# Row maxima per half of the queries: a hybrid layer's attention on one Trainium2 core

## The chip, the cores and the metric

The kernel runs on one core of one Trainium2 chip (trn2). The metric is the time of one execution on the device in microseconds. Engine names are those of the profile: PE multiplies matrices, DVE is the vector engine, ACT the scalar engine, POOL GpSimd, SP the engine that issues nearly all DMAs.

## What is computed

A residual stack over x of shape (2, 1024, 128): a gated linear recurrence with an MLP, a mixture of experts, an attention with a relative bias, and the same mixture again. Each takes the layer-normed x and is added to it. The change touches the attention, which has 16 heads of 8 channels (D = 128, scale 128 ** -0.5):

```python
q, k, v = (x @ W.T, split into 16 heads of 8, for Wq, Wk, Wv)
attn = softmax(q k^T * scale, axis=-1)
attn = attn + rel_bias_table[i - j + seq_len - 1]   # clipped to the table
out = attn @ v
out = (out - mean(out)) * rsqrt(var(out) + eps) * ln_gamma + ln_beta
```

## The kernel before, in words

Every engine has an instruction list of its own, written out by hand; semaphores order them. The first 200 us are dense layers. Then the attention runs in GROUPS = 8 groups of GH = 4 heads (four for each of the NB = 2 rows of the batch). Within a group the S = 1024 queries and keys are NT = 8 tiles of 128, and TH = 4 tiles make a half of 512.

Queries and keys are split into three bf16 parts each (L992 to L1005 on DVE, L637 on ACT, L528 on POOL), stored to `qk_scratch` (`store_parts`, L414) and loaded again, stacked to 72 rows (`load_products`, L423, 24 DMAs for a group: a query load L429 and a key load L430 for each of four heads and three parts), into one of BUFS = 3 buffers.

**Maxima.** For each head and query tile PE multiplies 128 queries by all 1024 keys into two PSUM banks (`max_item`, L1331, two matmuls of 512 columns, L1339), and DVE reduces them to minus the maximum (L1028). A group has MAXES = 32 of these. One transpose turns the 128 x 32 of them (`turn_maxes`, L1343), DVE splits them into three bf16 parts (`split_negmax`, L1030), and SP loads these as rows 72 to 74 under the queries (`load_negmax`, L432, three DMAs, L436), so that the scores come out with the maximum taken off.

**Scores.** A group has STEPS = 16 steps: two halves q of the queries, eight key tiles t in each. A step (`step`, L1420) is four score matmuls, one for each head (`scores`, L1393, L1402), with the exponentials on ACT (L731), and the weighing of the step before (`weigh`, L1405, L1416), which adds up in one bank. After eight steps ACT takes that bank (`take_pv`, L718, L721). The first score of a group waits for `negmax_loaded`.

**The ring.** Maxima, turns, the bias products (`bias_part`, L1347, L1353), their turn (`turn_bias`, L1357) and the output's turn (`turn_out`, L1362, eight transposes) share two PSUM slots of two banks each, in the order of the list RING (L190, 36 items); PE fills, DVE empties in the same order (`empty`, L1046). An item waits until the item two before it is emptied, a turn also until the last of its maxima is (`ring_needs`, L209). An item is (kind, d, k): it belongs to the group d after the one whose scores run. Share j of RING, `j * 36 // 16` to `(j + 1) * 36 // 16`, goes into step FIRST + j, FIRST = 2, so shares 14 and 15 lie in steps 0 and 1 of the next group. RING starts with maximum 10 of the next group; its turn is item 25, followed by maxima of the group after next (d = 2) up to EARLY = 10, and the output's turn is last. Ahead of the first score there are RING_AHEAD's 43 items (32 maxima of group 0, a turn, 10 maxima of group 1), between which the attention's projections of row 1 are placed (L1460 to L1477 on PE, L1076 to L1099 on DVE). Groups 6 and 7 run over shortened lists, since no further group follows: group 7 has no maxima beside it.

**SP's queue** (`round_`, L444) is, for each group G: wait until step 1 is scored, load the products of G + 2; wait for the bias table to be free, load that of G + 2; wait for the split maxima of G + 1, load them. SP works strictly in this order, as every engine does.

**Row 0's norm** after the attention (`attended_out`, `attended`, L1106 to L1125) runs on DVE at the end of group 6's list, and the mixture of row 0 begins beside group 7 (TURN_STEP, LOGITS_STEP, X_STEP, L206).

Of the kernel before, what the change touches and what calls it, by code (L numbers as in the profile page):

```python
# [28 lines left out]
BF16 = mybir.dt.bfloat16  # L29
ALU = mybir.AluOpType  # L30
# [76 lines left out]
def values(b):  # L107
    return [(f"V.{b}.{h}", "dve") for h in range(2)] + [(f"CS.{b}", "dve")]
# [73 lines left out]
MAXES = GH * NT  # L182
# [15 lines left out]
BIAS_AT = RING.index(("bias", 0, 0))  # L198

RING_BEFORE_LAST = [item for item in RING if item[1] < 2]  # L200
RING_LAST = [item for item in RING if item[1] < 1]

TURN_STEP, LOGITS_STEP, X_STEP = 4, 5, 10  # L206


def ring_needs(items, k):  # L209

    kind, d, _ = items[k]
    made_from = {"turn": ("max", d, MAXES - 1), "bias_turn": ("bias", d, 0)}.get(kind)
    return max(k - 1, items.index(made_from) + 1) if made_from in items else k - 1


def build(nc, x_in, out, w, tab):
    ctx = ExitStack()
    with ctx:
# [99 lines left out]
        qs = q_words.bitcast(BF16).rearrange("p (n h t) -> p n h t", n=BUFS, h=GH)  # L318
# [10 lines left out]
        nm_rest = sb("nm_rest", [GH * NT, P])  # L329
        nm_part = sb("nm_part", [GH * NT, NPART, P], BF16)  # L330
        rl = sb("rl", [P, NT, GH])
# [10 lines left out]
        def score_bank(g, n):  # L342
# [26 lines left out]
        PER_GROUP = {ring_filled: len(RING), ring_emptied: len(RING), negmax_split: 1, scores_filled: STEPS * GH,  # L369
                     exp_done: STEPS * GH, pv_done: STEPS, pv_out: 2, varying_ready: 1, v_ready: 1, negmax_loaded: 16 * NPART,  # L370
# [3 lines left out]
        RING_SHORT = len(RING) - len(RING_BEFORE_LAST)  # L374

        def at(G, s, k):

            short = RING_SHORT if s in (ring_filled, ring_emptied) and isinstance(G, int) and G == GROUPS - 1 else 0
            return G * PER_GROUP[s] + k + AHEAD.get(s, 0) - short
# [1170 lines left out]
```

## Time and profile before

| | |
|---|---|
| median of 3 runs | 740.3 us (738.14 to 742.24) |
| profiled execution, span | 738.4 us |
| PE busy | 666.5 us (90%) |
| DVE busy | 533.7 us (72%) |
| ACT busy | 381.2 us (52%) |
| POOL busy | 104.9 us (14%) |
| first score of the attention | 256.2 us from the span's start |
| last take of weighed values (L721) | 664.0 us |

The span is from the first to the last instruction of one execution that the hardware profiler recorded; its time as a run is not given apart from that; the lowest of the timed runs is 738.14 us. Busy time is the union of an engine's instructions. Matmuls are pipelined and their ends are modelled, so a busy PE is not PE at its peak. In a view of groups the idle time before a group's instructions stands last, with what ended most of it. In a timeline, a row merges instructions that follow each other on one engine; DMA-issuing instructions on SP's queue are shown as SPq. PEclk is the granted share of PE's 2.4 GHz.

### The profile page before, as it was taken

How to read it: one execution, taken by the hardware profiler on the slowest of the kernel's cores; microseconds unless marked ns; L12 is line 12 of the kernel's file. 1: busy time of each engine (PE TensorE's matmuls, PEld its weight loads, DVE VectorE, ACT ScalarE, POOL GpSimd, SP SyncE). 2: the span in 40 equal slices, each digit the busy share in tenths (PEclk: the TensorE clock that was granted, in tenths of full speed). 3: DMA queues.
4: the chain of work that ended last, by engine and by line, in shares of the span. 5: the costliest groups of instructions: out<-in, count | busy, mean ns of one | idle time of the engine just before them, and what ended most of it. 6: DMA issues, size and time to landing. Idle time of an engine off the chain costs nothing.

```text
span 738.4 us, 10515 instructions
## 1 busy us (share of the span) xinstructions
PE 666.5 (90%) x3192; PEld 254.5 (34%) x3192; DVE 533.7 (72%) x956; ACT 381.2 (52%) x687; POOL 104.9 (14%) x100
## 2 busy tenths in 40 slices
PE   3988898999777699999999899999999998988997
PEld 1434344444343222332322232332322322324443
DVE  5379788746699868868878768868788688308744
ACT  2745133333203057767767657766667677882231
POOL 5910110001044411020020020020100202002000
PEclk9998899999969789999999999999999999999999
DMA  8000000000313102012012020030120000000000
GB/s 253 5 1 0 1 0 1 1 0 0 112 67 122 58 28 95 2 41 83 4 56 66 17 83 28 18 99 9 32 91 3 2 0 2 2 1 0 1 28 28
DMA packets 21413, 26.59 MB, mean 36 GB/s; under 512 B 3312, under 2 KB 12016, under 8 KB 21360
## 3 DMA queue, kind: packets, MB, share of 16 engines
q1 hardware_dynamic: 20496, 25.39, 10.8%
q8 instruction: 29, 0.48, 0.3%
q0 software_dynamic: 144, 0.52, 0.2%
q14 instruction: 24, 0.20, 0.1%
q10 hardware_dynamic: 720, 0.00, 0.1%
HBM read 21.52 MB, written 4.19 MB: 35 GB/s over the span
## 4 chain that ended last, share of the span: by engine, by line
PE 69%; DVE 19%; ACT 4%; issue 2%; DMA 2%; DVEq 1%; POOL 1%; SPq 1%; POOLq 0%; ACTq 0%
PE banks L1416 17%; PE banks L1339 15%; PE banks L1402 14%; PE banks L1154 6%; DVE negmax L1028 6%; PE banks L1224 4%; PE banks L1265 3%; PE banks L1353 2%; PE banks L1215 2%; PE banks L1161 2%; DVE arena L886 1%; ACT arena L731 1%; DVE arena L936 1%; DVE stats L783 1%; PE banks L1366 1%
## 5 line engine op out<-in xcount | busy, mean ns | idle before, releaser
L1028 DVE TENSOR_REDUCE negmax<-banks 128x1 f32<-128x1024 f32 x256 | 300.8, 1217 | 68.6 <-PE banks L1339 67.4
L731 ACT ACTIVATE arena<-banks 128x512 f32<-128x512 f32 x512 | 271.7, 601 | 144.1 <-PE banks L1402 140.6
L1339 PE MATMUL banks<-arena 72*128 72x512 bf16 x512 | 161.3, 400 | 23.6 <-DVE negmax L1028 19.7
L1402 PE MATMUL banks<-arena 75*128 75x512 bf16 x512 | 160.2, 384 | 6.7 <-ACT arena L731 3.1
L1416 PE MATMUL banks<-arena 128*32 128x512 f32 x1024 | 138.1, 612 | 0.7 <-ACT arena L731 0.7
L1339 PEld LDWEIGHTS banks<-arena 72*128 72x128 bf16 x512 | 37.8, 100 | 163.0 <-DVE negmax L1028 77.0
L1402 PEld LDWEIGHTS banks<-arena 75*128 75x128 bf16 x512 | 48.6, 98 | 95.7 <-ACT arena L731 48.0
L495 POOL TENSOR_TENSOR rstd<-veps,neghalf 128x4 f32<-128x4 f32 (+1 forms) x24 | 27.1, 1129 | 247.3 <-DVE veps L802 192.1
L1224 PE MATMUL banks<-arena,bT 128*128 128x512 f32 x128 | 60.1, 593 | 1.6 <-ACT arena L585 1.6
L585 ACT ACTIVATE arena<-banks 128x512 f32<-128x512 f32 (+1 forms) x56 | 32.2, 595 | 53.1 <-PE banks L1154 22.7
L886 DVE TENSOR_SCALAR arena<-banks,bi 128x512 f32<-128x512 f32 x32 | 23.8, 745 | 34.7 <-PE banks L1224 34.7
L562 POOL TENSOR_TENSOR pause<-neghalf 128x8 f32<-128x8 f32 x7 | 1.4, 199 | 309.9 <-PE banks L1353 309.9
L1224 PEld LDWEIGHTS banks<-arena,bT 128*128 128x128 f32 x128 | 24.2, 190 | 32.2 <-issue 29.9
L1416 PEld LDWEIGHTS banks<-arena 128*32 128x32 f32 x1024 | 20.3, 108 | 39.3 <-issue 33.2
L1215 PE MATMUL banks<-hT,wiT 128*128 128x512 f32 x64 | 32.9, 615 | 0.0
L1161 PE MATMUL banks<-ident,nt 128*128 128x128 f32 x80 | 13.7, 313 | 20.4 <-DVE nt L812 11.9
L546 POOL TENSOR_TENSOR arena<-arena,t_last 128x2048 f32<-128x2048 f32 x8 | 28.8, 3599 | 0.0
L585 ACT ACTIVATE hT<-banks 128x512 f32<-128x512 f32 x12 | 6.8, 596 | 31.8 <-PE banks L1161 31.8
L1265 PE MATMUL banks<-arena,woT 128*128 128x512 f32 x48 | 22.1, 597 | 0.3
L585 ACT ACTIVATE x<-banks,bi 128x512 f32<-128x512 f32 x16 | 11.0, 687 | 20.3 <-PE banks L1224 20.3
L783 DVE BATCH_NORM_STATS2 stats<-x 128x6 f32<-128x128 f32 x80 | 17.4, 280 | 5.4 <-DMA x<-in_x 4.5
L585 ACT ACTIVATE oT<-banks,bo 128x512 f32<-128x512 f32 x8 | 5.5, 687 | 30.4 <-PE banks L1265 30.4
(128 smaller groups left out, 614.1 us busy)
## 6 DMA issues: line engine op xcount, KB each, us to landing
arena<-qk_scratch SPq DMA_DIRECT2D x192, 48.0 KB
arena<-in_tab SPq DMA_DIRECT2D x8, 1024.0 KB, 6.8
qk_scratch<-arena SPq DMA_DIRECT2D x8, 384.0 KB, 2.8
out<-x SPq DMA_DIRECT2D x4, 256.0 KB, 2.3
x<-in_x SPq DMA_DIRECT2D x1, 512.0 KB, 4.5
x<-in_x POOLq DMA_DIRECT2D x1, 512.0 KB, 7.7
arena<-nm_part SPq DMA_DIRECT2D x24, 8.0 KB, 1.9
w_aT<-in_w_aT SPq DMA_DIRECT2D x1, 256.0 KB, 6.5
```

Source lines behind the costliest of these rows:

```text
L546: pool.tensor_tensor(varying, bias_raw[:, :, ::-1], t_last[:, bass.ds(G * GH, GH)].unsqueeze(2).broadcast_to([P, GH, BIASW]), ALU.subtract ...
L585: act.activation(dst, banks[:, BANK[name], :], func, **kw).then_inc(signal or act_emptied, 1)
L731: act.activation(probs[s % 2][:, h, :], score_bank(g, n), ACT.Exp, scale=SCALE).then_inc(exp_done, 1)
L886: dve.tensor_scalar(h1[:, c % 2, :], bank(name), bi[:, c:c + 1], 0.0, ALU.add, ALU.max).then_inc(dve_emptied, 1)
L1028: return dve.tensor_reduce(negmax[:, buf, k:k + 1], slot.rearrange("p a b -> p (a b)"), axis=AXX, op=ALU.max, negate=True)
L1154: last = pe.matmul(banks[:, BANK[name], :], lhsT, rhs, start=i == 0, stop=i == len(terms) - 1)
L1215: pe.matmul(banks[:, BANK[name], :], chunk(wiT, c), half(hT[:, b], h), start=True, stop=False, skip_group_check=True)
L1224: pe.matmul(banks[:, BANK[name], :], chunk(bT, c), half(moe[b][4][:, k, :], h), start=False, stop=k == 1, skip_group_check=True).then_inc( ...
L1265: last = pe.matmul(banks[:, BANK[name], :], woT[:, c, :], moe[b][2][h][:, c, :], start=c == 0, stop=c == FC - 1)
L1339: last = pe.matmul(slot[:, half_, :], qs[0:STACK, buf, h, t * P:(t + 1) * P], ks[0:STACK, buf, h, half_ * HALF:(half_ + 1) * HALF], start= ...
L1402: pe.matmul(score_bank(g, n), ks[0:DEPTH, g % BUFS, h, t * P:(t + 1) * P], qs[0:DEPTH, g % BUFS, h, q * HALF:(q + 1) * HALF], start=True, ...
L1416: last = pe.matmul(pv_bank[32 * h:32 * h + VW, :], vpg[:, g % BUFS, t, h, :], probs[s % 2][:, h, :], start=t == 0, stop=t == NT - 1)
```

## The change

The maxima of a group are taken, turned, split and loaded for each half of the queries: MAXES is 16, and item k of 32 is maximum `k % 16` of half `k // 16`. Each group has two turns of 128 x 16, two splits and two times three loads. The first score of each half waits for its own loads. The queries lie as (half, head, 512) in their buffer, and the query loads write two pieces of 1 KB a row instead of one of 2 KB. The second half's maxima of a group from EARLY = 8 on, and its turn, are now beside that group's own scores (d = 0); no item has d = 2. RING has 38 items, RING_AHEAD 25. The output is turned in two halves (items 33 and 37). In SP's order the second half's loads stand behind the product loads. Groups 6 and 7: group 6 has the whole list, group 7 has eight maxima, a turn, the bias and the outputs, three items a step; row 0's norm is done tile by tile between their items. The value copies of the projections go from DVE to ACT, and POOL clears `vpg` and copies the first values ahead of its low parts.

```diff
-MAXES = GH * NT
+MAXES = GH * TH
-EARLY = 10
+EARLY = 8
-NEXT_MAXES = [("max", 1, k) for k in range(EARLY, MAXES)]
-AFTER_NEXT = [("max", 2, 0), ("turn", 1, 0)] + [("max", 2, k) for k in range(1, EARLY)]
-RING = NEXT_MAXES[:4] + [("bias", 0, 0), NEXT_MAXES[4], ("bias_turn", 0, 0)] + NEXT_MAXES[5:] + AFTER_NEXT + [("out", 0, 0)]
-RING_AHEAD = [("max", 1, k) for k in range(MAXES)] + AFTER_NEXT
-BESIDE_FIRST = EARLY - 4
-R_BEFORE, V0_BEFORE, CS0_BEFORE = 2, (4, 5), 7
-TURN_BEFORE, QK_BEFORE, V_BEFORE, CS_BEFORE = 12, (14, 16, 18, 20), (22, 24), 27
+def maxes(d, q, start, stop):
+    return [("max", d, q * MAXES + k) for k in range(start, stop)]
+TURN_0 = maxes(1, 0, 0, 1) + [("turn", 0, 1)] + maxes(1, 0, 1, 3) + BIAS + maxes(1, 0, 3, 4) + BIAS_TURN + maxes(1, 0, 4, MAXES)
+AFTER_TURN = maxes(1, 1, 0, 1) + [("turn", 1, 0)] + maxes(1, 1, 1, EARLY)
+RING = maxes(0, 1, EARLY, MAXES) + TURN_0 + AFTER_TURN[:6] + [("out", 0, 0)] + AFTER_TURN[6:] + [("out", 0, 1)]
+RING_AHEAD = maxes(1, 0, 0, MAXES) + AFTER_TURN
+BESIDE_FIRST = 4
+R_BEFORE, V0_BEFORE, CS0_BEFORE = 2, (3, 4), 5
+TURN_BEFORE, QK_BEFORE, V_BEFORE, CS_BEFORE = 8, (10, 11, 12, 13), (14, 15), 17
+RING_LAST = maxes(0, 1, EARLY, MAXES - 1) + BIAS + maxes(0, 1, MAXES - 1, MAXES) + BIAS_TURN + [("turn", 0, 1), ("out", 0, 0), ("out", 0, 1)]
+LAST_BESIDE = 3
-TURN_STEP, LOGITS_STEP, X_STEP = 4, 5, 10
+TURN_STEP, LOGITS_STEP, X_STEP = 8, 9, 14
...
-            def load_negmax(G, buf):
-                sp.wait_ge(negmax_split, at(G, negmax_split, 1))
+            def load_negmax(G, buf, q):
+                sp.wait_ge(negmax_split, at(G, negmax_split, q + 1))
                 for i in range(NPART):
...
                     sp.wait_ge(scores_filled, at(G, scores_filled, FIRST * GH))
                     load_products(G + 2, (n + 2) % BUFS)
+                load_negmax(G, n % BUFS, 1)
+                if left >= 2:
                     sp.wait_ge(varying_ready, at(G, varying_ready, 2))
                     load_bias(G + 2)
                 if left >= 1:
-                    load_negmax(G + 1, (n + 1) % BUFS)
+                    load_negmax(G + 1, (n + 1) % BUFS, 0)
...
             store_parts(1)
+            load_negmax(0, 0, 0)
+            sp.wait_ge(qk_stored[1], 64)
             sp.wait_ge(varying_ready, 1)
             load_bias(1)
-            load_negmax(0, 0)
...
-                if n == 0:
-                    pe.wait_ge(negmax_loaded, at(G, negmax_loaded, 16 * NPART))
+                if s % NT == 0 and h == 0:
+                    pe.wait_ge(negmax_loaded, at(G, negmax_loaded, (s // NT + 1) * 16 * NPART))
...
+            def round_before_last():
+                G = GROUPS - 2
+                for k, item in enumerate(RING):
+                    dve.wait_ge(ring_filled, at(G, ring_filled, k + 1))
+                    empty(G, G, item, ring_slot(k))
+                    if k in (TH, 2 * TH):
+                        stats_half(N_OUT, 0, o_tok, k // TH - 1)
+                    if NT < k <= 2 * NT:
+                        if k == NT + 1:
+                            dve.drain()
+                        centred(0, k - NT - 1)
...
+                act.activation(v_all[:, b * NG:(b + 1) * NG, h * TH:(h + 1) * TH, :],
+                               banks[:, BANK[name], :].rearrange("p (t g c) -> p g t c", g=NG, c=GW), ACT.Copy).then_inc(act_emptied, 1)
```

## Rows read from the trace of the kernel before

**Rows 1.** The page: span, and busy time, share and instructions of two engines.

```profile
span 738.4 us, 10515 instructions
...
PE 666.5 (90%) x3192; PEld 254.5 (34%) x3192; DVE 533.7 (72%) x956; ACT 381.2 (52%) x687; POOL 104.9 (14%) x100
```

**Rows 2.** The reductions' group: count, busy, mean ns, idle before, releaser.

```profile
L1028 DVE TENSOR_REDUCE negmax<-banks 128x1 f32<-128x1024 f32 x256 | 300.8, 1217 | 68.6 <-PE banks L1339 67.4
```

**Rows 3.** Timeline, PE, steady stretch: start, length, line, op.

```profile
350.79 1.06 PE L1416 MATMUL banks<-arena 128*32 128x512 f32 x8
...
353.63 1.06 PE L1416 MATMUL banks<-arena 128*32 128x512 f32 x8
...
356.61 1.07 PE L1416 MATMUL banks<-arena 128*32 128x512 f32 x8
```

**Rows 4.** Timelines: first score of step 8 (group 2); seven takes.

```profile
387.73 0.60 PE L1402 MATMUL banks<-arena 75*128 75x512 bf16 x2
...
363.50 0.60 ACT L721 ACTIVATE arena<-banks 128x512 f32<-128x512 f32 x1
...
390.25 0.60 ACT L721 ACTIVATE arena<-banks 128x512 f32<-128x512 f32 x1
...
414.22 0.60 ACT L721 ACTIVATE arena<-banks 128x512 f32<-128x512 f32 x1
...
444.85 0.60 ACT L721 ACTIVATE arena<-banks 128x512 f32<-128x512 f32 x1
...
570.25 0.60 ACT L721 ACTIVATE arena<-banks 128x512 f32<-128x512 f32 x1
...
620.23 0.60 ACT L721 ACTIVATE arena<-banks 128x512 f32<-128x512 f32 x1
...
664.03 0.60 ACT L721 ACTIVATE arena<-banks 128x512 f32<-128x512 f32 x1 [1.19 <-PE banks L1416]
```

**Rows 5.** Timeline of SP's queue, groups 1 and 2.

```profile
356.27 1.86 SPq L436 DMA_DIRECT2D arena<-nm_part  x3
...
367.23 0.82 SPq L429 DMA_DIRECT2D arena<-qk_scratch  x1
...
388.53 0.39 SPq L441 DMA_DIRECT2D arena<-in_tab  x1
```

**Rows 6.** The turn in group 1; time to landing of nm_part loads.

```profile
354.62 0.28 PE L1345 MATMUL banks<-ident,negmax 128*32 128x128 f32 x1
...
DMA to landing us min/median/max: 1.8/1.9/3.2
```

**Rows 7.** Windows, last columns PEclk, DMA share, GB/s: product loads; three nm_part loads.

```profile
373.00:387.00 14.00, 13.55 (x98) 4.40 (x98) 8.88 (x10) 8.22 (x17) 4.09 (x3) 1.00 0.18 58
...
357.00:359.00 2.00, 2.00 (x14) 0.52 (x7) 2.00 (x3) 1.12 (x4) 0.00 (x0) 1.00 0.06 12
```

**Rows 8.** PE after a gap of 2.29 us; PEclk in two windows.

```profile
420.91 0.39 PE L1402 MATMUL banks<-arena 75*128 75x512 bf16 x1 [2.29 <-issue]
...
422.00:424.00 2.00, 2.00 (x10) 0.25 (x10) 0.99 (x1) 1.07 (x2) 0.00 (x0) 0.51 0.19 54
...
260.00:262.00 2.00, 2.00 (x6) 0.68 (x5) 1.89 (x3) 0.97 (x2) 0.00 (x0) 0.50 0.00 0
```

**Rows 9.** Timelines of the stage ahead of the scores, 210 to 256 us.

```profile
210.05 6.22 POOL L524 TENSOR_SCALAR nt<-x,mv,rstd 128x128 f32<-128x128 f32 x8
...
229.49 7.70 SPq L419 DMA_DIRECT2D qk_scratch<-arena  x4
...
237.08 0.68 DVE L1009 COPY x<-banks 128x512 f32<-128x512 f32 x1
...
256.17 0.59 PE L1402 MATMUL banks<-arena 75*128 75x512 bf16 x1 [1.09 <-DMA arena<-nm_part]
```

**Rows 10.** Timeline of DVE in the last group: norm work of row 0.

```profile
612.97 0.87 DVE L783 BATCH_NORM_STATS2 stats<-z 128x6 f32<-128x128 f32 x4
...
615.92 2.18 DVE L1112 SCALAR_TENSOR_TENSOR nt<-z,mv,gamma 128x128 f32<-128x128 f32 x8
```

More of the change, by code:

```diff
@@ L1092, in _ @@
                 rest(1, k)
-            for h in range(2):
-                empty_ahead(done, V_BEFORE[h])
-                done = V_BEFORE[h]
-                take_values(1, h)
-            empty_ahead(done, CS_BEFORE)
+            empty_ahead(done, CS_EMPTY)
             take_sum(1)
-            empty_ahead(CS_BEFORE, len(RING_AHEAD))
-            def round_items(G, g, items, first=0):
-                for k, item in enumerate(items, first):
+            empty_ahead(CS_EMPTY, len(RING_AHEAD))
@@ L1103, in round_items @@
+            def round_items(G, g, items):
+                for k, item in enumerate(items):
                     dve.wait_ge(ring_filled, at(G, ring_filled, k + 1))
                     empty(G, g, item, ring_slot(k))
-            def attended_out(b):
-                dve.drain()
-                for h in range(2):
-                    stats_half(N_OUT, b, o_tok, h)
-                for t in range(NT):
-                    dve.scalar_tensor_tensor(out=nt[:, b, t, :].rearrange("p (g c) -> p g c", g=NG), in0=tile_of(o_tok, b, t),
-                                             scalar=mv[:, b, t, 0:1], in1=gamma[:].rearrange("p (g c) -> p g c", g=NG),
-                                             op0=ALU.subtract, op1=ALU.mult)
@@ new lines, in last_round @@
+            def last_round():
+                G = GROUPS - 1
+                dve.wait_ge(x_beta, 1)
+                for k, item in enumerate(RING_LAST[:LAST_OUT]):
+                    dve.wait_ge(ring_filled, at(G, ring_filled, k + 1))
+                    empty(G, G, item, ring_slot(k))
+                    if k < NT:
+                        attended_tile(0, k)
+                norm(N_FFN1, 0, x)
+                route(1, 0)
+                for k in range(LAST_OUT, len(RING_LAST)):
+                    dve.wait_ge(ring_filled, at(G, ring_filled, k + 1))
+                    empty(G, G, RING_LAST[k], last_slot(k))
@@ L1360, in turn_bias, with turn_out @@
                 return last
-            def turn_out(G, slot):
-                pe.wait_ge(pv_out, at(G, pv_out, 2))
-                for t in range(NT):
-                    last = pe.transpose(slot[:, t // TH, (t % TH) * P:(t % TH + 1) * P], chunk(pvT, t), ident[:])
+            def turn_out(G, slot, q):
+                pe.wait_ge(pv_out, at(G, pv_out, q + 1))
+                for t in range(TH):
+                    last = pe.transpose(slot[:, 0, t * P:(t + 1) * P], chunk(pvT, q * TH + t), ident[:])
                 return last
@@ L1435, in step, with beside @@
                     fill_item(k)
-            def beside(items, j):
-                share = RING[j * len(RING) // STEPS:(j + 1) * len(RING) // STEPS]
-                return [items.index(x) for x in share if x in items]
+            def beside(j):
+                return list(range(j * len(RING) // STEPS, (j + 1) * len(RING) // STEPS))
             def round_(G, g, items):
@@ L1447, in round_ @@
                     s = FIRST + j
-                    step(G + s // STEPS, g + s // STEPS, s % STEPS, fill_item, beside(items, j))
+                    step(G + s // STEPS, g + s // STEPS, s % STEPS, fill_item, beside(j))
             for name in LAST_IN_RING:
@@ L1486, in _ @@
                     round_(i * BUFS + n, n, RING)
-            round_(GROUPS - 2, GROUPS - 2, RING_BEFORE_LAST)
+            round_(GROUPS - 2, GROUPS - 2, RING)
             G = GROUPS - 1
             def fill_last(k):
-                fill_round(G, G, RING_LAST, k)
+                pe.wait_ge(ring_emptied, at(G, ring_emptied, ring_needs(RING_LAST, k)))
+                fill(G, G, RING_LAST[k], last_slot(k))
             for j in range(STEPS - FIRST):
                 s = FIRST + j
-                step(G, G, s, fill_last, [j] if j < 2 else [])
+                step(G, G, s, fill_last, list(range(j * LAST_BESIDE, min((j + 1) * LAST_BESIDE, LAST_OUT))))
                 if s == TURN_STEP:
-                    pe.wait_ge(ring_emptied, at(G, ring_emptied, 2))
+                    pe.wait_ge(ring_emptied, at(G, ring_emptied, LAST_OUT))
                     flip_norm(N_FFN1, 0, "T1")
```

145 lines of the change are left out of this document (75 added, 70 removed).

## The prediction

> **What bounds the kernel now.** I read the page first: in the profiled execution of 738.4 us PE is busy 90% and DVE 72% [rows 1]. Those are averages over stages with different limits, so I then went through timelines. The group of the reductions shows what DVE does with its share: 256 maxima of 1.22 us each, 300.8 us [rows 2]. In the middle of a group of heads the bursts of weighing (L1416) stand 2.84 us apart, and 2.98 us where the turn lies between them [rows 3]. A step there holds four scores and two items of maxima, eight matmuls of 512 columns, 1.7 us at 2.4 GHz, and the burst, close to 1 us: PE is full. ACT needs 4 x 0.6 us for it and DVE two maxima; neither is the bound. A group takes 50.7 us: 26.8 us from the take of step 0 to that of step 8 (the bias products lie in this half), 24.0 us for the other half; group 3 is 3.9 us longer in its first half, 30.6 us [rows 4]. Ahead of the first score DVE reduces 42 maxima without a pause, and PE waits on it: that stage is DVE's.
>
> **SP's queue** is what the change leans on. It issues the 24 loads of products for group 2's successor but one from 367.23 to 388.53, 21.3 us, 0.89 us each, and is then free for the next thing [rows 5]. The three loads of split maxima come 1.65 us after the turn on PE; issuing them takes 1.9 us, a load lands 1.9 us after its issue, so the last one is there about 3.15 us after the first issue [rows 5, 6]. Before the change they start at 356.27, eleven microseconds ahead of the products, and nobody waits for them.
>
> **The change, part by part.**
>
> *Shorter stage ahead of the scores.* The list falls from 43 items to 25, 18 reductions less. DVE also loses four value copies of 0.68 us [rows 9] to ACT, which idles there; behind them on ACT stand the turns of row 1, not ready before POOL has finished its norm at 216.3 [rows 9], and for row 1 nothing but the first exponentials. The limit by DVE alone is 18 x 1.22 + 2.7 = 24.7 us. But the chain of row 1 remains. Its turn stands at item 8 instead of 12 and so starts about 4 us earlier; between its four products stands one maximum instead of two, 3 x 1.2 = 3.6 us less. SP's last store of parts, finished at 237.2 [rows 9], moves to about 229.5. The value sum, two maxima, the turn and the split follow, 3 us, then 3.15 us of loads, and about 1 us for the stores still in flight (the slowest landing of such a load is 3.2 us against 1.9 [rows 6]): the first score comes at 236.5 instead of 256.2, 19.7 us earlier. POOL's clearing and its first two value copies move ahead of its low parts, into time in which it waited for these. On SP the first loads of maxima move ahead of the wait for the stores and of the table load, which takes that wait off the path. The first two steps carry four items instead of six at the low clock: 2 x 2 x 512 columns at 1.2 GHz are 1.7 us, of which I take 1.3. Sum -21, bounds -25 and -13 (the chain of row 1 not shortened at all).
>
> *The second half's loads behind the products.* In SP's order the loads of the second half's maxima stand behind the 24 product loads of the group after next. These start, now as before, when step 1 has been scored. Step 8 needs the maxima. In group 2 step 8's first score came at 387.95 (the second matmul of the row at 387.73 [rows 4]), 20.7 us after the first product load; the new order has one item more before it but only half of an output turn, the same within 0.3 us. The maxima are there after 21.3 + 3.15 = 24.5 us. PE, whose queue is in order, stands for about 4.0 us at that score, with every item, weighing and exponential behind it. Groups 0, 1, 2, 4 and 5 pay this; group 3 has 3.9 us more in the loop's turn-round, so 0.3 us; groups 6 and 7 load no products. Behind the loads of maxima SP has the table load, which POOL needs only a group later, so nobody waits for that. 5 x 4.0 + 0.3 = +20.3. Bounds per group: 3.2 (a queue 0.8 us faster) and 5.3 (the landing of 3.2 us).
>
> *The clock.* After a gap of 2.29 us on PE the granted clock of 422 to 424 us is 0.51, that is 1.2 GHz, with the engine full [rows 8]. That half group lost 3.9 us: the gap and some 1.5 us for the clock. A gap of 4 us should do no less: 5 x 1.5 = +7.5. Bounds 0 and 3.4 each: at the start the clock stays at 0.50 although PE is full [rows 8], and 1.2 steps of 2.84 us run at half the clock take 3.4 us more.
>
> *Work moved to the last two groups.* The 18 maxima come back in groups 6 and 7 (50.0 and 43.8 us now [rows 4]). PE is the bound there or nearly so, an item is two times 512 columns at 2.4 GHz, 0.43 us: 7.7 us. In group 7 three maxima share a step, with a tile of the norm behind each (2.18 us for eight [rows 10]): DVE needs 4.2 us for such a step, about 1 us more than PE, twice. The norm of row 0, until now 10 us of DVE between the groups' items, is strewn over groups 6 and 7 (four statistics are 0.87 us, eight tiles 2.18 us [rows 10]) and takes the slack that DVE has there; its turn and logits stand four steps later, still ahead of the end of group 7. Sum +9.5, bounds 7.7 and 14.
>
> *In each of seven groups* there is one turn more and the output turn is in two: 0.15 us for a turn [rows 3], the same for the split of the output. The turn of the first half now stands two steps ahead of its use instead of three: 5.7 us against 1.65 + 3.15 and a reduction in front, so no slack; 0.2 us. 7 x 0.5 = +3.5, bounds 0 and 10. *The last output* in two halves puts 0.6 us on the tail (-0.3 to 1).
>
> Sum: -21 + 20.3 + 7.5 + 9.5 + 3.5 + 0.6 = +20.4 on the execution of 738.4 us. The runs' median, 740.3, stands 1.9 us above it, so 760.7, rounded to 761.
>
> **A rule that bears on it.** The product loads hold the DMA share at 0.18 for 14 us on end, with nothing else moving [rows 7]; 3 of 16 engines are 0.19. They seem to use three engines only, and to fill them. The Trainium skill says that an outermost dimension of size c below 16, such as a leading broadcast, confines a DMA to at most c engines (DMA: Bandwidth & Descriptors, Rules for kernel authors); by that rule, the trace agrees. That gives a rival. A packet of 2 KB costs 0.18 x 14 x 16 / (15.8 loads x 24) = 0.106 us of one engine; the 96 small packets of the three loads of maxima 0.06 x 2 x 16 / 96 = 0.02 us each [rows 7]. The query loads now have 48 pieces of 1 KB instead of 24 of 2 KB. On the line between both rows 1 KB costs 0.057 us, and a pair of loads 1.76 us on three engines against 1.78 us of issue: just hidden, which I take. At 0.106 us for 1 KB too it is 2.54 us a pair, and after 12 pairs 9 us of backlog lie in front of the maxima.
>
> **The rivals.** *Three engines back up* (chance 0.12): for it, they are full today; against it, small packets are cheap in the rows. Half of the 9 us in five groups and a little in group 3: 761 + 24 = 785, up to 810.
>
> *The maxima arrive in time* (0.13), and the kernel gets faster. The place is SP's queue in groups 0 to 5; it decides at 17.5 us for the 24 product loads, 0.73 us each. Then +20.3 and +7.5 drop out: 761 - 27.8 = 733. For it speaks only that the issue itself is shown as 0.82 us at most and that the rest of the 0.89 us may be address arithmetic; against it, this pitch holds in every group seen.
>
> *The stage ahead does not get shorter as counted* (0.08): row 1's chain through POOL, ACT, DVE and SP bounds it from the start; the first score comes at 245, and the time is 769. *The stall is there but cheap* (0.05): no clock loss and the full 25 us at the start, 744 and less.
>
> **How the numbers follow.** The forecast gets 0.62: its stall is a matter of order in one queue, and its own range is 748 to 774. From 743 to 785 the range takes in the third rival and half of the backed-up engines; left out are the arrival in time (0.13) and the rest of the backlog (0.06). A measurement of this kernel can tell some 0.5% from no change, 3.7 us. Faster 0.13, the arrival in time; same 0.05, the cheap stall; slower 0.82.
>
> **What would show it.** First score near 236. In the waits, PE's scores released by the loads of nm_part, 4 us in five groups and nearly nothing in the fourth. In SP's queue, the three loads of maxima directly behind the 24 of products, once a group, and three more later. PEclk at 0.5 for some us after each gap. First halves of 32 us instead of 26.8. If first halves stay at 27, my step on SP's queue is wrong, and the kernel is faster.

## The result, and the profile after

The kernel got slower: 786.8 us median of 4 runs (784.08 to 794.84) against 739.56 us for the kernel before in the same runs (738.14 to 742.24), a ratio of 1.064, 95% interval 1.059 to 1.069. The forecast was 761, in a range up to 785: the direction was right, the size was not. Here and below, a ratio leaves out runs that took over 1.5% longer than the fastest run of the same kernel. The profiled execution took 788.15 us, 786.2 of them its span; before it was 738.4 [rows 1], so 47.8 us are to be found. The page of the changed kernel: span, busy time by engine, the granted clock in 40 slices, and the chain that ended last by engine.

```profile
span 786.2 us, 10702 instructions
...
PE 689.5 (88%) x3200; PEld 262.7 (33%) x3200; DVE 548.1 (70%) x1000; ACT 387.0 (49%) x691; POOL 104.9 (13%) x100
...
PEclk9998899999796999899999999989979979999999
...
PE 54%; DVE 19%; SPq 14%; issue 4%; ACT 3%; DMA 3%; DVEq 2%; POOL 1%; POOLq 0%; ACTq 0%
```

SP's queue now holds 14% of the chain, though the data that the kernel needs are the same. PE's busy time rose by 23 us [rows 1] for eight more matmuls. Most of that is the same work at a lower clock: over the span the clock is at half for 101 us, against 57 before. To see where, I cut the attention at three events: the first score, the take of group 6's step 0, and group 7's last take.

| stretch, us | before | after | change |
|---|---|---|---|
| start of the span to the first score | 256.2 | 237.8 | -18.3 |
| groups 0 to 5: first score to that take | 314.1 | 364.4 | +50.3 |
| groups 6 and 7: that take to the last | 93.8 | 109.7 | +15.9 |
| last take to the end | 74.4 | 74.3 | 0.0 |

The takes of the changed kernel (the timeline of ACT, whose line is L747 now) answer to [rows 4]. In this list stand, in order: step 8 of group 0, steps 0 and 8 of groups 1 and 2, step 8 of group 3 and step 0 of group 4, step 0 of group 6, and the last take.

```profile
275.80 0.60 ACT L747 ACTIVATE arena<-banks 128x512 f32<-128x512 f32 x1 [1.04 <-PE banks L1449]
...
301.68 0.60 ACT L747 ACTIVATE arena<-banks 128x512 f32<-128x512 f32 x1 [0.16 <-PE banks L1449]
335.15 0.60 ACT L747 ACTIVATE arena<-banks 128x512 f32<-128x512 f32 x1 [1.24 <-PE banks L1449]
361.91 0.60 ACT L747 ACTIVATE arena<-banks 128x512 f32<-128x512 f32 x1 [0.16 <-PE banks L1449]
394.06 0.60 ACT L747 ACTIVATE arena<-banks 128x512 f32<-128x512 f32 x1 [1.24 <-PE banks L1449]
...
452.96 0.60 ACT L747 ACTIVATE arena<-banks 128x512 f32<-128x512 f32 x1 [0.16 <-PE banks L1449]
478.85 0.60 ACT L747 ACTIVATE arena<-banks 128x512 f32<-128x512 f32 x1 [0.16 <-PE banks L1449]
...
602.18 0.60 ACT L747 ACTIVATE arena<-banks 128x512 f32<-128x512 f32 x1 [0.15 <-PE banks L1449]
...
711.86 0.60 ACT L747 ACTIVATE arena<-banks 128x512 f32<-128x512 f32 x1 [1.19 <-PE banks L1449]
```

The first half of group 1 takes 33.47 us (301.68 to 335.15), that of group 2 32.15; before they took 26.75. The second half of group 1 takes 26.76, and that of group 3, which no wait and no low clock disturbs, 25.89; before, 23.97. **Both** kinds of halves became longer, and the wait that was foreseen lies in the first kind alone.

That wait is there as forecast. The first score, and then group 1 on SP, on DVE (the last step of the split) and on PE, from the timelines:

```profile
237.83 0.59 PE L1435 MATMUL banks<-arena 75*128 75x512 bf16 x1 [1.32 <-DMA arena<-nm_part]
...
305.40 0.84 SPq L439 DMA_DIRECT2D arena<-qk_scratch  x1
...
326.55 0.72 SPq L440 DMA_DIRECT2D arena<-qk_scratch  x1
327.41 1.85 SPq L446 DMA_DIRECT2D arena<-nm_part  x3
...
320.62 0.28 DVE L1061 TENSOR_TENSOR nm_part<-nm_rest,nm_part 16x128 bf16<-16x128 f32 x1
...
325.88 0.60 PE L1372 MATMUL banks<-arena 72*128 72x512 bf16 x2
330.90 0.60 PE L1435 MATMUL banks<-arena 75*128 75x512 bf16 x1 [4.43 <-DMA arena<-nm_part]
```

DVE had the second half's maxima split at 320.9. SP was in the middle of the 24 product loads and came to them at 327.4, 22.0 us after the first product load. PE stood for 4.43 us. The 24 issues themselves took at most 0.3 us longer than before (22.0 us in this group, 22.1 before; 21.5 to 21.9 in the others, 21.3 to 21.6 before). The sum over all groups, from the chain of waits (us in total, times, longest):

```profile
PE banks L1435 <- DMA arena<-nm_part: 20.3, 6, 4.4
```

1.3 of the 20.3 us are at the first score; groups 0, 1, 2, 4 and 5 pay 2.6, 4.4, 3.9, 4.3 and 3.8, and group 3 nothing. What follows the waits is, in sum, more than the forecast allowed. PE behind the wait of group 4, timeline and windows (busy PE, PEld, DVE, ACT, POOL, then PEclk, DMA share, GB/s):

```profile
507.98 0.60 PE L1435 MATMUL banks<-arena 75*128 75x512 bf16 x1 [4.34 <-DMA arena<-nm_part]
...
512.09 1.03 PE L1372 MATMUL banks<-arena 72*128 72x512 bf16 x2
```

```profile
511.00:513.00 2.00, 2.00 (x11) 0.37 (x4) 0.00 (x0) 0.60 (x1) 0.00 (x0) 0.50 0.26 99
...
515.00:517.00 2.00, 2.00 (x10) 0.20 (x8) 1.09 (x1) 1.08 (x2) 0.00 (x0) 0.50 0.00 0
```

PE is busy 2.00 of 2.00 us in each of these windows and is granted 0.50, that is 1.2 GHz; two matmuls of 512 columns take 1.03 us, where the group 1 rows above show 0.60 for the same two. The low stretches at the five waits last 3.4, 6.8, 3.4, 10.2 and 10.2 us; 32.3 us of them lie behind the waits, where PE works. Half of that is lost: 16.2 us.

19.0 of waits and 16.2 of clock leave 15.1 of the 50.3 us. Most of it lies in the ring. A step whose items are three maxima, timelines of PE and DVE, group 1:

```profile
337.72 1.06 PE L1449 MATMUL banks<-arena 128*32 128x512 f32 x8
...
340.64 0.61 PE L1372 MATMUL banks<-arena 72*128 72x512 bf16 x2 [0.45 <-DVE negmax L1050]
...
341.61 0.64 PE L1449 MATMUL banks<-arena 128*32 128x512 f32 x4
...
339.36 3.49 DVE L1050 TENSOR_REDUCE negmax<-banks 128x1 f32<-128x1024 f32 x3 [0.74 <-PE banks L1372]
```

From one weighing to the next there are 3.89 us instead of 2.84 [rows 3]: three reductions are 3.5 us of DVE and PE waits for the bank. With 36 items in 16 steps, the ring before had four steps of three items, and one of these held three maxima; with 38 items there are six, and four hold three maxima, three of the four in the second half. Two more of them at 1.05 us are 2.1 us, about the 1.9 by which an undisturbed second half is longer (25.89 against 23.97): 11.5 us in six groups. Of the rest, 1.9 us lie in the first half of group 3, where the loop turns round: the clock is low there for 6.8 us, against 3.4 before.

Group 6 has an accident of its own. Timelines of POOL, DVE and PE:

```profile
628.04 3.60 POOL L567 TENSOR_TENSOR arena<-arena,t_last 128x2048 f32<-128x2048 f32 x1
...
628.44 3.34 DVE L1120 SCALAR_TENSOR_TENSOR nt<-z,mv,gamma 128x128 f32<-128x128 f32 x1
...
632.84 0.34 DVE L1120 SCALAR_TENSOR_TENSOR nt<-z,mv,gamma 128x128 f32<-128x128 f32 x1
...
632.97 0.60 PE L1372 MATMUL banks<-arena 72*128 72x512 bf16 x2 [2.31 <-DVE negmax L1050]
```

The norm's tile that takes 0.34 us took 3.34 beside POOL's bias product and ended 0.14 us behind it (631.78 and 631.64). The maxima behind it came late and PE stood 2.31 us; from 0.8 us later on the granted clock was 0.50 for 10.2 us. Group 6's second half took 32.43 us.

### The profile page after: what moved, and what is told of

It reads as the page before. It is cut to its first block, busy times and chain, and to the rows that moved or that the text cites. A ratio compares the mean times of both kernels' runs of the same rounds, so it can differ in the third digit from the quotient of the medians.

```text
span 786.2 us, 10702 instructions
## 1 busy us (share of the span) xinstructions
PE 689.5 (88%) x3200; PEld 262.7 (33%) x3200; DVE 548.1 (70%) x1000; ACT 387.0 (49%) x691; POOL 104.9 (13%) x100
## 3 DMA queue, kind: packets, MB, share of 16 engines
q1 hardware_dynamic: 23184, 25.39, 10.2%
## 4 chain that ended last, share of the span: by engine, by line
PE 54%; DVE 19%; SPq 14%; issue 4%; ACT 3%; DMA 3%; DVEq 2%; POOL 1%; POOLq 0%; ACTq 0%
PE banks L1449 13%; PE banks L1372 11%; PE banks L1435 10%; DVE negmax L1050 7%; SPq L439 7%; SPq L440 6%; PE banks L1187 6%; PE banks L1257 4%; PE banks L1248 3%; PE banks L1298 2%; DMA arena<-nm_part 2%; PE banks L1194 2%; ACT arena L757 2%; DVE stats L809 1%; DVE arena L962 1%
## 5 line engine op out<-in xcount | busy, mean ns | idle before, releaser
L757 ACT ACTIVATE arena<-banks 128x512 f32<-128x512 f32 x512 | 275.2, 600 | 188.3 <-PE banks L1435 184.1
L1435 PE MATMUL banks<-arena 75*128 75x512 bf16 x512 | 172.5, 402 | 26.9 <-DMA arena<-nm_part 20.3
L1372 PE MATMUL banks<-arena 72*128 72x512 bf16 x512 | 164.8, 406 | 27.2 <-DVE negmax L1050 23.7
L1449 PE MATMUL banks<-arena 128*32 128x512 f32 x1024 | 146.9, 648 | 1.0 <-ACT arena L757 1.0
L1372 PEld LDWEIGHTS banks<-arena 72*128 72x128 bf16 x512 | 39.5, 101 | 174.7 <-issue 77.2
L1435 PEld LDWEIGHTS banks<-arena 75*128 75x128 bf16 x512 | 51.6, 102 | 115.0 <-ACT arena L757 38.9
L602 ACT ACTIVATE arena<-banks 128x512 f32<-128x512 f32 (+1 forms) x56 | 32.2, 595 | 48.4 <-PE banks L1194 19.5
L1257 PEld LDWEIGHTS banks<-arena,bT 128*128 128x128 f32 x128 | 24.2, 190 | 32.3 <-issue 29.9
L1194 PE MATMUL banks<-ident,nt 128*128 128x128 f32 x80 | 13.0, 300 | 20.8 <-DVE nt L838 12.1
L1298 PE MATMUL banks<-arena,woT 128*128 128x512 f32 x48 | 22.1, 597 | 0.3
L602 ACT ACTIVATE x<-banks,bi 128x512 f32<-128x512 f32 x16 | 11.0, 687 | 21.9 <-PE banks L1257 21.9
L809 DVE BATCH_NORM_STATS2 stats<-x 128x6 f32<-128x128 f32 x80 | 17.4, 280 | 5.6 <-DMA x<-in_x 4.6
L602 ACT ACTIVATE arena<-banks,bi 128x512 f32<-128x512 f32 x16 | 11.0, 687 | 16.8 <-PE banks L1257 16.8
```

The source lines that it names most:

```text
L602: act.activation(dst, banks[:, BANK[name], :], func, **kw).then_inc(signal or act_emptied, 1)
L757: act.activation(probs[s % 2][:, h, :], score_bank(g, n), ACT.Exp, scale=SCALE).then_inc(exp_done, 1)
L1257: pe.matmul(banks[:, BANK[name], :], chunk(bT, c), half(moe[b][4][:, k, :], h), start=False, stop=k == 1, skip_group_check=True).then_inc( ...
L1298: last = pe.matmul(banks[:, BANK[name], :], woT[:, c, :], moe[b][2][h][:, c, :], start=c == 0, stop=c == FC - 1)
L1372: last = pe.matmul(slot[:, half_, :], qs[0:STACK, buf, q, h, t * P:(t + 1) * P], ks[0:STACK, buf, h, half_ * HALF:(half_ + 1) * HALF], sta ...
L1435: pe.matmul(score_bank(g, n), ks[0:DEPTH, g % BUFS, h, t * P:(t + 1) * P], qs[0:DEPTH, g % BUFS, q, h, :], start=True, stop=True).then_inc ...
```

## The experiments

The theory to test (A): one misplaced line in SP's order costs the waits; the clock behind them costs about as much again; the ring's three-maxima steps and the norm in group 6 cost the rest. Rivals: the longer queue or the smaller pieces of the loads slow everything (backed-up engines), or the time beyond the waits is work that piled up, not clock. Two remarks on all comparisons. Each ratio is against runs of the kernel before that were taken beside it (medians 744.11 us in experiments 1, 4 and 5, 740.54 in 3, 740.55 in 6 to 9), and the profiled execution was the fastest of its runs in experiments 4, 6, 7 and 8, up to 8 us below the median. And the first maximum of the stage ahead of the scores starts at 202.1 us in the execution shown above, and between 196.7 and 202.4 in the others, through the clock granted to the dense stages before it; in experiments 8 and 9 the first score is therefore also given from the first maximum.

**1. The second half's loads ahead of the products.**

```diff
+                load_negmax(G, n % BUFS, 1)
                 if left >= 2:
                     sp.wait_ge(scores_filled, at(G, scores_filled, FIRST * GH))
                     load_products(G + 2, (n + 2) % BUFS)
-                load_negmax(G, n % BUFS, 1)
-                if left >= 2:
```

> The changed kernel with one edit: SP loads the second half's maxima of group G ahead of the 24 product loads of G+2. Theory A (the stall at step 8 and the low clock that follows it come from SP's order): the waits of PE for nm_part, 19.0 us in all, go to under 2, PEclk stays at 1.0 there (it was at 0.5 for about 33 us in groups 0 to 5, some 16 us lost), and the time falls by about 35 us to 751. Rival B (the low clock is there anyway, by the lighter load on PE): only the 19 us go, 768. Rival C (the loads are late for another reason, the transfer engines being full): no change, 787.

752.59 us (752.35 to 758.5), ratio 1.017 (1.007 to 1.026). The waits of the changed kernel with this order:

```profile
PE banks L1434 <- DMA arena<-nm_part: 5.5, 5, 3.1
```

3.1 us are at the first score. None of the others, 0.5 to 0.7 us, is at a step 8: they are at the first scores of groups 1, 2, 5 and 6. First halves are 27.0 us (31.2 in group 3), second halves 25.9 to 26.1, groups 0 to 5 together 328.4 us instead of 364.4. The waits fell by 16.6 us (19.0 to 2.4) and the stretch by 36.0: each microsecond of waiting had cost another. So 34 us of the loss hang on this line's place, as theory A had it (751). Of the 14.3 us by which the stretch is still longer than before the change, 12.1 lie in the second halves, where the ring has its steps of three maxima. Groups 6 and 7 take 114.5 us here, 4.8 more than in the changed kernel: the accident of group 6 is dearer in this run (its second half takes 35.69 us, with the clock at half for 17.1).

**2. A dose of it: 22 of the 24 product loads ahead.**

```diff
-            def load_products(G, buf):
+            def load_products(G, buf, pairs=range(GH * NPART)):
...
+                        if h * NPART + i not in pairs:
+                            continue
...
-                    load_products(G + 2, (n + 2) % BUFS)
+                    load_products(G + 2, (n + 2) % BUFS, range(11))
                 load_negmax(G, n % BUFS, 1)
                 if left >= 2:
+                    load_products(G + 2, (n + 2) % BUFS, range(11, GH * NPART))
```

> The changed kernel with 22 of the 24 product loads ahead of the second half's maxima and 2 behind them, so every gap at step 8 is 1.8 us shorter: 0.8, 2.6, 2.1, 2.5, 2.0 us in groups 0, 1, 2, 4, 5 instead of 2.6, 4.4, 3.9, 4.3, 3.8. Theory A: each gap shrinks by just that, 8.9 us in all; if the clock still falls after gaps of 2 us, 778; if it does not, 765. Rival C (transfer engines full): the maxima land no earlier, 787.

One run: 759.01 us, span 757.1. The waits of groups 0, 1, 2, 4 and 5 are 1.0, 2.6, 2.1, 2.0 and 1.9 us, 1.6 to 2.3 less for two loads less, where the pitch of 0.89 us says 1.8. The stretch of groups 0 to 5 is 342.6 us, 14.2 over experiment 1 for 7.2 us more of waiting (9.6 against 2.4): twice, again, but only in sum. The granted clock is 0.50 from 321.1 to 324.6 and from 379.2 to 386.0 us, behind the waits of groups 1 and 2, and does not fall behind those of groups 4 and 5: a gap of 2 us lowers it in some places and in others not. Groups 4 and 5 are 2.0 and 1.7 us longer than in experiment 1, no more than their waits; groups 1 and 2 are 4.3 and 5.5 us longer. The time lies below both marks that I had set, by things that these marks left out (against the execution of the changed kernel the first score is 4.6 us earlier, and groups 6 and 7 take 2.7 us less), so this run settles the dose and not the clock's price.

**3. The gap filled with matmuls.** The sharpest test of the clock: the wait stays, PE is kept busy in it. The condition on g holds for groups 1, 2, 4 and 5.

```diff
+                if s == NT and h == 0 and g < BUFS and g > 0:
+                    pe.wait_ge(exp_done, at(G, exp_done, n - 2))
+                    for _ in range(16):
+                        pe.matmul(score_bank(g, n), ks[0:STACK, g % BUFS, h, 0:P], qs[0:STACK, g % BUFS, 1, h, :],
+                                  start=True, stop=True)
                 if s % NT == 0 and h == 0:
                     pe.wait_ge(negmax_loaded, at(G, negmax_loaded, (s // NT + 1) * 16 * NPART))
```

> The kernel after with one thing added: in groups 1, 2, 4 and 5, PE runs 16 matmuls of 512 columns on the loaded queries and keys into the bank of the next score, right before it waits for the second half's maxima, and the score then overwrites them. They leave nothing out and take 16 x 0.216 = 3.5 us of the 3.8 to 4.4 us in which PE stands there. Theory A (the gap itself costs what its length is, and a low clock afterwards costs as much again or nearly): the loads land as before, so the stall of about 4 us a group stays, now filled, but the granted clock stays near 1.00 behind it in these groups. After, it was 0.50 for 6.3, 3.1, 10.1 and 10.1 us behind the four gaps, 29.6 us, half of it lost: 14.8 us. So 786.8 - 14.8 = 772, with first halves of groups 1, 2, 4, 5 near 31 (26.8 + 4) and second halves 25.9. Rival B (the time beyond the gap is work that piled up behind the wait, exponentials and maxima that have to be caught up, whatever the clock): the halves stay at 32.2 to 33.5 and 28.6, and the time at 787. Rival C (the clock falls later anyway, since what lowers it is not the gap): also near 787, with PEclk 0.5 in the same stretches.

771.45 us (770.64 to 775.33), ratio 1.044 (1.036 to 1.052), against 772 by theory A and 787 by the rivals. PE in group 1, timeline, and a window over the first half of group 4, whose gap lies at 500 us here:

```profile
325.19 3.62 PE L1432 MATMUL banks<-arena 72*128 72x512 bf16 x16
329.33 0.39 PE L1440 MATMUL banks<-arena 75*128 75x512 bf16 x1 [0.52 <-DMA arena<-nm_part]
```

```profile
490.00:520.00 30.00, 28.24 (x178) 9.44 (x171) 19.44 (x21) 16.48 (x31) 4.10 (x3) 1.00 0.16 53
```

The first halves of groups 1, 2, 4 and 5 became 31.1, 30.6, 31.4 and 31.4 us (33.5, 32.2, 33.4 and 32.8 without the filling) and all four second halves are 25.9 (26.8, 26.3, 28.6 and 28.6): 14.0 us back, though PE still does nothing useful in these four gaps. The exponentials and maxima that had to wait are the same, so "work that piled up" falls. Group 0, whose gap was not filled, shows the other side in the same execution: its wait is 5.5 us, and the clock is low from 267.9 to 274.8 us. The clock's price is shown: 14.5 us for the four groups, half of the 28.9 us in which PE worked at the low clock (the expectation had 14.8), and 14.0 measured.

**4. The norm of row 0 later in group 6**, behind POOL's product (items 20 to 27 of the ring).

```diff
-                    if NT < k <= 2 * NT:
-                        if k == NT + 1:
+                    if 20 <= k < 20 + NT:
+                        if k == 20:
                             dve.drain()
-                        centred(0, k - NT - 1)
+                        centred(0, k - 20)
```

> The changed kernel with row 0's centred tiles in group 6 moved from items 9 to 16 to items 20 to 27, where POOL's long operation is over. Theory A (one 0.34 us operation of DVE took 3.34 us beside POOL's 3.6 us one, PE stood 2.3 us for it and its clock fell for 10 us): group 6's second half goes from 32.4 to about 26 us and the time to 780. Rival B (DVE has too much work there, wherever it stands): it stays at 32, 787.

782.03 us (773.71 to 784.57), ratio 1.055 (1.046 to 1.064), against 780 by theory A. The takes on either side of group 6's second half:

```profile
622.38 0.60 ACT L747 ACTIVATE arena<-banks 128x512 f32<-128x512 f32 x1 [0.22 <-PE banks L1449]
...
648.30 0.60 ACT L747 ACTIVATE arena<-banks 128x512 f32<-128x512 f32 x1 [0.16 <-PE banks L1449]
```

It went from 32.43 to 25.92 us, groups 6 and 7 together from 109.7 to 102.8. The place in DVE's order was the cause; nothing of the norm is left out. The slow tile is no chance event: in the traces of experiments 1, 2, 3 and 5, which leave the norm where it was, one tile takes 3.34 us beside POOL's product, as in the changed kernel; in those with the norm later (4, 6, 7 and 8) all eight take 0.33 to 0.35 us.

**5. The ring without three-maxima steps.** The bias and its turn stand one and two items later, and the shares of the steps are written by hand.

```diff
-TURN_0 = maxes(1, 0, 0, 1) + [("turn", 0, 1)] + maxes(1, 0, 1, 3) + BIAS + maxes(1, 0, 3, 4) + BIAS_TURN + maxes(1, 0, 4, MAXES)
+TURN_0 = maxes(1, 0, 0, 1) + [("turn", 0, 1)] + maxes(1, 0, 1, 4) + BIAS + maxes(1, 0, 4, 6) + BIAS_TURN + maxes(1, 0, 6, MAXES)
+SHARES = [2] * 4 + [3] * 3 + [2] * 5 + [3] + [2] + [3] * 2
...
-                return list(range(j * len(RING) // STEPS, (j + 1) * len(RING) // STEPS))
+                return list(range(sum(SHARES[:j]), sum(SHARES[:j + 1])))
```

> The changed kernel with the ring rearranged so that each of the 16 steps holds exactly two maxima, and the six light items (turns, bias, outputs) are each the third of a step; same items, same instructions. Now four steps of a group hold three maxima and take 3.9 us instead of 2.84. Theory A (a step with three maxima is DVE's and costs about 1.05 us more): three of these lie in the second halves and save 3.1 us in each of seven groups, those in the first half vanish in the stall at step 8: 763. Rival B (the sum of the work counts, not its packing): 787.

785.74 us (784.26 to 787.13), ratio 1.059 (1.050 to 1.068): a miss by 23 us. The stretch of groups 0 to 5 did fall, from 364.4 to 355.5, and second halves are 25.2 instead of 25.9 or more. Two timelines of PE say why it isn't more:

```profile
358.63 0.39 PE L1436 MATMUL banks<-arena 75*128 75x512 bf16 x1 [0.90 <-DMA arena<-nm_part]
...
390.43 0.39 PE L1436 MATMUL banks<-arena 75*128 75x512 bf16 x1 [4.54 <-DMA arena<-nm_part]
```

The first half's loads, whose turn stands two steps ahead, are now 0.9 us late (a second half without that is 24.3, nearly the 23.96 of before). At step 8 nothing can be won at all: the loads land when SP gets to them, so a faster ring waits longer, 4.1 to 4.9 us in groups 1, 2, 4 and 5. The waits rose from 20.3 to 31.0 us in 13 places. Groups 6 and 7 gave back another 5.8 us, in the kind of collision that experiment 4 removes (35.47 us for group 6's second half).

**6. Order and norm together.**

> The two edits together: SP's order, and row 0's centred tiles at items 20 to 27 of group 6. With SP's order alone group 6's second half took 35.7 us, against 25.9 for the others. Theory A (DVE's operation beside POOL's, and the low clock behind it): it goes to 26, so 752.6 - 9.7 = 743. Rival B (work on DVE): 752.

The edits are those of experiments 1 and 4. 747.67 us (742.47 to 752.09, 10 runs), ratio 1.010 (1.006 to 1.013), 5 us over the forecast. Groups 0 to 5 take 329.8 us in the profiled execution, groups 6 and 7 102.8 instead of 114.5 with the order alone.

**7. All three.**

> SP's order, the later norm and the ring with two maxima in every step. Without SP's stall the packing can show in both halves: halves of 27.0 and 25.9 us in the kernel with SP's order go to 26.0 and 25.2, less what the turn's loads cost, 0.9 us per group in the first try. Theory A: 12 halves x 0.8 us less than the kernel with order and norm alone, so about 734. Rival B (each saved step comes back as a wait for the turn's loads, two steps behind it): 743.

766.07 us (760.18 to 768.91), ratio 1.035 (1.028 to 1.042): 18 us **worse** than without the third, far from theory A (734) and from rival B (743), and the largest miss. SP and PE between groups 1 and 2, and a window:

```profile
336.62 0.41 SPq L452 DMA_DIRECT2D arena<-in_tab  x1
338.86 1.85 SPq L447 DMA_DIRECT2D arena<-nm_part  x3
...
343.78 0.60 PE L1435 MATMUL banks<-arena 75*128 75x512 bf16 x1 [2.76 <-DMA arena<-nm_part]
```

```profile
338.00:340.00 2.00, 2.00 (x14) 0.47 (x12) 1.83 (x5) 1.86 (x4) 0.00 (x0) 1.00 0.82 247
...
344.00:350.00 6.00, 6.00 (x21) 2.06 (x21) 1.93 (x4) 2.81 (x5) 0.00 (x0) 0.52 0.01 1
```

SP issues the 1 MB load of the table 2.2 us ahead of the first half's loads of maxima. These share the engines with it (DMA share 0.82) and the score comes 4.9 us after their issue instead of about 3.2, as by [rows 6]. In each of groups 1 to 6 the last of the three lands 0.5 us behind the table (343.7 and 343.1 us here); in experiment 6 too, but there the steps ahead of this score are slower, and PE gets to it later. In the execution shown eight scores beside the first wait, 0.6 to 3.5 us, 17.4 us in all, the clock falls at five of them, and halves of 25.5 to 29.4 us follow (group 3's first half aside). In experiment 6 it is four scores and 2.1 us. Two of the eight waits (0.6 us at step 8 of group 2, 2.4 us at the first score of group 7) have no table load ahead of them: their last load landed 3.95 and 3.31 us after its issue, and why stays open.

**8. The turns three steps ahead.** EARLY is 10 again, as in the kernel before; the rest as in experiment 7, with the first output item three items later.

```diff
-EARLY = 8
+EARLY = 10
...
+SHARES = [2] * 3 + [3] * 3 + [2] * 5 + [3] + [2] * 2 + [3] * 2
...
-RING = maxes(0, 1, EARLY, MAXES) + TURN_0 + AFTER_TURN[:6] + [("out", 0, 0)] + AFTER_TURN[6:] + [("out", 0, 1)]
+RING = maxes(0, 1, EARLY, MAXES) + TURN_0 + AFTER_TURN[:9] + [("out", 0, 0)] + AFTER_TURN[9:] + [("out", 0, 1)]
```

> As the last, with EARLY = 10: two more maxima of each group ahead of its scores, so that both turns stand three steps ahead of their use as in the kernel before. Theory A: the waits of 0.9 us for nm_part in every group go, at the price of two more items ahead of the first score (2.3 us, part of it covered): 731, ahead of both kernels. Rival B (waits of that size are hidden elsewhere): 734 to 736.

736.07 us (733.37 to 740.32, 10 runs) against 740.55 for the kernel before (19 runs): ratio 0.995 (0.991 to 0.999), the only version of the changed scheme that isn't slower. It gains half a per cent, and the value copies of experiment 9 are part of it. No score waits for maxima any more. Takes of group 2:

```profile
342.32 0.60 ACT L747 ACTIVATE arena<-banks 128x512 f32<-128x512 f32 x1 [0.16 <-PE banks L1449]
...
370.90 0.60 ACT L747 ACTIVATE arena<-banks 128x512 f32<-128x512 f32 x1 [0.16 <-PE banks L1449]
```

Its first half is 28.58 us and its second 22.90, 51.5 a group, against 52.9 in experiment 1 and 50.7 before. With the ring dealt out and no wait left, 0.8 us a group remain for the added items. Groups 0 to 5 take 317.5 us (314.1 before), groups 6 and 7 103.1 (93.8), and the stage from the first maximum to the first score 36.1 (53.7).

**9. The value copies alone**, put on ACT in the kernel before.

```diff
-    return [(f"V.{b}.{h}", "dve") for h in range(2)] + [(f"CS.{b}", "dve")]
+    return [(f"V.{b}.{h}", "act") for h in range(2)] + [(f"CS.{b}", "dve")]
...
```

The copies themselves move with it, from DVE's list to ACT's, ahead of and behind the products of row 1.

> The kernel before with one part of the change alone: the four value copies on ACT instead of DVE. Theory A (the stage ahead is DVE's): 4 x 0.68 us less, the first score at 253.5, ratio 0.996. Rival B (the chain of row 1 or the transfers bound it): the first score stays at 256.2, ratio 1.000.

734.57 us (733.0 to 744.1), ratio 0.989 (0.981 to 0.997). The first score comes at 249.97 instead of 256.17, but the first maximum too comes 5.0 us earlier. From the one to the other there are 52.6 us instead of 53.7: 1.2 us (52.55 against 53.72) is the copies' own, between theory A's 2.7 and the rival's nothing. The 5 us are from stages that the edit does not touch. Windows of the kernel before, then of this one, 80 to 120 us, with PEclk third from the right:

```profile
80.00:120.00 40.00, 37.83 (x121) 19.29 (x120) 30.42 (x91) 10.33 (x18) 6.44 (x5) 0.95 0.00 1
```

```profile
80.00:120.00 40.00, 35.98 (x123) 18.39 (x121) 32.29 (x101) 11.57 (x20) 6.44 (x5) 1.00 0.00 1
```

Whether the copies' place has part in that clock stays open: the two levels of these stages occur with several edits, and the interval reaches to 0.997. Experiment 8's kernel, which has this edit in it, is at 736.07 us no faster than this one: no run shows that the maxima by halves gain anything of their own.

## Why the prediction was right or wrong

Its terms against the 47.8 us (the 3.5 us for seven groups are split over two rows):

| step | forecast | measured |
|---|---|---|
| stage ahead of the scores | -21 (-25 to -13) | -18.3 |
| waits in groups 0 to 5 | +20.3 | +19.0 |
| clock behind them | +7.5 (0 to 17) | +16.2 |
| rest of groups 0 to 5: turns, outputs | +3 (0 to 9) | +15.1 |
| groups 6 and 7 | +10 | +15.9 |
| last output | +0.6 | 0.0 |

**SP's queue: right.** The order of the queue, the pitch of 0.89 us, the landing, the wait of about 4 us at step 8, its near absence in group 3 and 24 loads as its cause all came out as read from [rows 5, 6]; experiments 1 and 2 move the wait by the loads that they move. In group 0 the wait is only 2.6 us.

**The start: right within 3 us.** In the execution shown the first score came at 237.83, forecast for 236.5. DVE lost about this difference to POOL, in the split of the first maxima: a cast that takes 0.21 us elsewhere took 1.90 beside a sum on POOL and ended 0.08 us behind it. SP had issued the stores by 232.8 and waited for the split until 234.12, 1.3 us.

```profile
229.02 4.64 POOL L563 TENSOR_TENSOR x<-x,beta 128x1024 f32<-128x1024 f32 x2
...
231.84 1.90 DVE L1059 CAST nm_part<-nm_rest 16x128 bf16<-16x128 f32 x1
```

The 1.3 us that the first two steps were to save did not show: with the order mended, 33.3 us lie between the first score and the take of step 8 of group 0, and 32.6 before.

**The clock: the mechanism right, the term mis-sized.** "A gap of 4 us should do no less: 5 x 1.5" took the one gap of [rows 8] as a price for each. The term measured 16.2 us, close to the upper end of 17; for the four gaps that experiment 3 filled it is 14.5, and 14.0 came back. One gap was no basis for a middle value, as the low stretches spread from 3 to 10 us.

**"In each of seven groups ... 7 x 0.5 = +3.5": this is the step that failed.** It counted what the added turn and the split output cost PE, and not how 38 items fall on 16 steps. The steps are in the code and each maximum is 1.22 us of DVE [rows 2], so a step of three maxima is at least 3.7 us against 2.84 (it measured 3.89): I had worked this out for group 7, and not for the ring. It is 1.9 us for each of the second halves in groups 0 to 5, 11.5 us where 3 were forecast for everything, and with the rest 15.1, past the upper bound of 9 for these groups. Experiment 5 dealt the ring out evenly and won 0.7 us of the 1.9, 0.9 being lost to loads that were late; experiment 8, with the turns a step earlier too, has second halves of 22.9 us. There some of the work moved into the first halves, and what is left over the kernel before, 0.8 us a group, is near the 0.5 that this term had for the items themselves.

**Groups 6 and 7: right but for a collision.** With the norm behind POOL's product they take 102.8 us, 9.0 more than before; 9.5 was forecast, and 0.5 for group 6's share of the next term. The other 6.9 us are the one slow tile and the clock behind it. I had said that the norm takes the slack that DVE has there, without looking at what POOL does at that time.

**The rivals.** Backed-up engines: not seen. The product loads kept their pitch, the loads of maxima land in a median of 1.7 us against 1.9 [rows 6], right behind the product loads they take 1.9 to 2.3 us, and with the smaller pieces still in place experiment 1 took the waits at step 8 away. The time beyond 785 has another cause. The maxima in time: no; that kernel is experiment 1, and it comes to 752.6, not to 733, for the ring's and group 6's sake. The stage ahead was shortened nearly as counted, so that rival falls. The cheap stall: no, it cost its length again in clock; and its time, "744 and less", is not what the terms give, which with -25 at the start and no clock loss come to 749. The misses of the table add up: 2.7 at the start, 8.7 of clock, 12.1 in the rest of groups 0 to 5 and 5.9 in the last groups, less 1.3 of waits and 0.6 at the end, are within rounding the 27.4 us between the forecast's sum and the span.

## What to carry to other kernels

Before moving a transfer, write down what its queue issues ahead of it and when that is done; here the transfer needed 3 us and the 24 issues ahead of it 21. When items are added to a hand-dealt ring, deal them out again and price every step by its busiest engine, not by the mean; but mend the wait that is set from outside first, for a faster ring in front of it only waits longer, and one with less reserve can be slower (experiments 5 and 7). The gaps of 2.6 to 4.4 us on PE cost about twice their length in sum, and one by one from 1.4 to 2.3 times; a price for such a gap needs that range.

## What the runs showed of the hardware

At a gap of 4.3 us the granted clock fell to 0.50 for 10.2 us, and in the 9.7 of them that lie behind the gap PE was busy throughout; at gaps of 4.4 and 3.9 us the low stretch was 6.8 and 3.4 us long. A gap of 2.31 us was enough for 10.2 us in group 6; in experiment 2 a gap of 2.1 us was enough for 6.8, and gaps of 2.0 and 1.9 us did nothing. Sixteen matmuls whose results are thrown away, in the gaps of four groups, kept it at 1.00. I had expected a low stretch of about 3 us each time.

How long the clock stays low differs from run to run behind one and the same event, and with it what the event costs. Where the slow tile stands in group 6, its second half took 29.7 and 29.8 us with a low stretch of 3.4 (experiments 3 and 2), 32.4 with 10.2 (the changed kernel) and 35.7 with 17.1 (experiment 1), against 25.9 without the event.

A DVE instruction of 0.34 us took 3.34 beside a POOL product of 3.60 us on two inputs, and ended with it, in all five traces that have it beside the product. A DVE cast with one input, 0.21 us elsewhere, took 1.90 beside a POOL sum and ended with it too. The Trainium skill says that GpSimd shares its SBUF interfaces with VectorE and contends with DVE instructions that have two SBUF inputs (GPSIMD Engine Reference, Specifications); the slow tile reads z and gamma, and the trace agrees.

Three loads of 4 KB each land late when a load of 1 MB has been issued 1.9 to 3.4 us ahead on the same queue: the last of them lands 0.5 us behind the big one, in six of six groups of experiment 7. With 2.2 us it was 4.9 us from the first issue to the score, against 3.5 in the group 1 rows above.
